# Another order of the same steps on every engine of a four-stage graph network kernel

## What is computed

```python
h = relu(layernorm(x)); x = x + L0(h, adj)   # two layers: softmax of h.h^T, masked; three products with weights
h = relu(layernorm(x)); x = x + L1(h, adj)   # two layers: two bilinear scores, masked exp; one linear product
h = relu(layernorm(x)); x = x + L2(h, adj)   # attention, 12 heads of 32, bias 2*adj, output projection
h = relu(layernorm(x)); x = x + L3(h, adj)   # attention, 12 heads of 32, masked by adj
```

## Time and profile before

| what | value |
|---|---|
| time, median of 3 runs | 2900.89 us (2900.38 to 2901.71) |
| the profiled execution's own time | 2899.22 us |
| its span, first to last instruction | 2897.5 us |
| granted TensorE clock, mean | 0.995 |
| PE busy | 2794.9 us (96%) |
| DVE busy | 2424.7 us (84%) |
| ACT busy | 2116.5 us (73%) |
| POOL busy | 846.4 us (29%) |

### The profile page before, as it was taken

How to read it: one execution, slowest core, us unless ns; L and a number is a source line. 1 busy time by engine, 2 the same in 40 slices (tenths; PEclk the granted TensorE clock), 3 DMA queues, 4 the chain that set the end, 5 groups by cost and what they waited for, 6 DMA issues and landing times.

```text
span 2897.5 us, 87504 instructions
## 1 busy us (share of the span) xinstructions
PE 2794.9 (96%) x33735; PEld 2130.6 (74%) x33735; DVE 2424.7 (84%) x7450; ACT 2116.5 (73%) x6036; POOL 846.4 (29%) x1227
## 2 busy tenths in 40 slices
PE   6999999999999999999999999999999999999998
PEld 4777777777777777777777777677777777777787
DVE  5788888888888888898888888888888888888884
ACT  5677777777777777777677777777777777777763
POOL 0133233233233233233232332232332332332331
PEclk8999999999999999999999999999999999999999
DMA  6132232232232232232232322322322222322222
GB/s 220 21 56 45 50 54 45 52 53 46 52 55 44 52 54 45 52 56 43 51 49 46 55 47 49 54 46 48 57 45 49 57 47 47 57 44 49 54 50 42
DMA packets 458222, 154.85 MB, mean 53 GB/s; under 512 B 415312, under 2 KB 457808, under 8 KB 457808
## 3 DMA queue, kind: packets, MB, share of 16 engines
q1 hardware_dynamic: 457808, 149.25, 27.2%
HBM read 35.92 MB, written 12.58 MB: 17 GB/s over the span
## 4 chain that ended last, share of the span: by engine, by line
PE 64%; DVE 17%; DMA 8%; issue 4%; POOL 4%; SPq 2%; ACT 1%; DVEq 0%; POOLq 0%; ACTq 0%
PE bank_c L374 23%; PE bank_a L374 13%; PE bank_b L374 13%; DMA pt_halves<-prob_halves 7%; PE bank_c L548 4%; DVE score L1064 4%; PE bank_b L406 3%; POOL prob_halves L1220 2%; DVE neg_head_max L1069 2%; PE bank_c L420 2%; SPq L315 2%; PE bank_b L413 1%; DVE scaled_b L995 1%; PE bank_b L420 1%; POOL rstd_c L1171 1%
## 5 line engine op out<-in xcount | busy, mean ns | idle before, releaser
L1220 POOL TENSOR_TENSOR prob_halves<-prob,prob_halves 128x384 f16<-128x384 f32 x512 | 473.7, 930 | 597.7 <-DVE prob_halves L1079 597.6
L785 ACT ACTIVATE prob<-score,neg_head_max 128x128 f32<-128x128 f32 x1536 | 494.8, 390 | 56.5 <-DVE neg_head_max L1069 54.6
L1064 DVE SCALAR_TENSOR_TENSOR score<-bank_c,bias 128x384 f32<-128x384 f32 x512 | 281.8, 550 | 212.8 <-PE bank_c L548 202.7
L374 PE MATMUL bank_c<-htc_hi,w_lo 128*128 128x128 f16 x2304 | 405.4, 219 | 0.0
L374 PE MATMUL bank_c<-htc_lo,w_hi 128*128 128x128 f16 x2304 | 405.4, 219 | 0.0
L374 PE MATMUL bank_c<-htc_hi,w_hi 128*128 128x128 f16 x2304 | 405.4, 219 | 0.0
L374 PE MATMUL bank_a<-w_hi,hta_hi 128*128 128x384 f16 x1152 | 375.4, 326 | 0.7
L374 PE MATMUL bank_a<-w_lo,hta_hi 128*128 128x384 f16 x1152 | 375.4, 326 | 0.0
L1069 DVE TENSOR_REDUCE neg_head_max<-score 128x3 f32<-128x384 f32 x512 | 280.0, 547 | 2.4
L374 PE MATMUL bank_a<-w_hi,hta_lo 128*128 128x384 f16 x1152 | 250.3, 326 | 0.0
L374 PEld LDWEIGHTS bank_c<-htc_lo,w_hi 128*128 128x128 f16 x2304 | 225.4, 98 | 13.8
(11 more groups left out here) (202 smaller groups left out, 8991.2 us busy)
## 6 DMA issues: line engine op xcount, KB each, us to landing
x_in<-x SPq DMA_DIRECT2D x64, 192.0 KB, 2.4
out<-y_out SPq DMA_DIRECT2D x64, 192.0 KB, 2.4
pt_halves<-prob_halves SPq DMA_TRANSPOSE x512, 2.8
w_stage<-w_t SPq DMA_DIRECT2D x11, 576.0 KB, 5.7
adj_in<-adj SPq DMA_DIRECT2D x64, 64.0 KB, 2.1
adj_t<-adj_turned SPq DMA_DIRECT2D x64, 64.0 KB, 2.2
score<-w_t SPq DMA_DIRECT2D x4, 576.0 KB, 7.3
prob<-w_t SPq DMA_DIRECT2D x4, 576.0 KB, 7.5
```

The costliest lines, as they stand in the source:

```text
L374: mm = nc.tensor.matmul(out_ap, a, b, start=first and i == 0, stop=last and i == len(pairs_of) - 1, skip_group_check=True)
L785: ex = nc.scalar.activation(prob[:, j, c, :], score[:, j, c, :], ACT.Exp, bias=neg_head_max[:, j, c:c + 1])
L1064: V.scalar_tensor_tensor(score[:, j, :, :], chunked(c_banks[j][:, 0:D]), scale, bias[:, :].unsqueeze(1).to_broadcast([128, CHUNKS, 128]), ...
L1220: P.tensor_tensor(prob_halves[:, j, 1, :, :], prob[:, j, :, :], prob_halves[:, j, 0, :, :], ALU.subtract)\
```

## The change

The same steps run; `ORDER`, `FIRST`, `SPLITS`, `WARM_FIRST` and `WARM_LAST` are written anew. `WARM_START` stays 110. No generator, buffer, wait or instruction form changes. The idle matmuls are 225 and 806 (232 and 745 before).

The period's string of PE begins at another place. Turned so that both begin at the same step, with the moved letters apart, they read as follows (`-` before, `+` after):

```diff
-b y a yyyyyyyxx c   xxxxxabx tx yyyy b yaybyay wwtbwwwwxxaxx cc xx c x cacbax c x ccaw cwyybwwbwwc
+b y   yyyyyyyxx a c xxxxxabt xx yy a y b yybyay wwtbwwwwxxaxx ccc xxx cabacxx ccc aw cwyybwwbwwc
```

The diff:

```diff
 ORDER = {
-    "pe": "cwyybwwbwwcbyayyyyyyyxxcxxxxxabxtxyyyybyaybyaywwtbwwwwxxaxxccxxcxcacbaxcxccaw",
-    "act": "gwenwmicnwbjccjccjnbcbfjcgkbxccbakeknakeewebcwcwccqbbfagexipbaeieib",
-    "dve": "bbpbipppaipbabbbabcjbcacccjbccbjhaccnabhaqbkacbabaxnbhhakbbabbbaacaccbcchcchaczhhzbbpaazaa"
-           "apaaipbabxp",
-    "pool": "bmbhmnqahhbhhhhhaac",
-    "sp": "lsttttttttu",
+    "pe": "byyyyyyyyxxacxxxxxabtxxyyaybyybyayywwtbwwwwxxaxxcccxxxcabacxxcccawcwyybwwbwwc",
+    "act": "micnwbcwjcjnccjbnqbgjfckcbxckbaekcakeewebcwcwnccbbgfaxeibpiaeeigbwe",
+    "dve": "bpppaipbbbbbcjabcaacjccjcbcbccaqaaabkbabbhcxbhakbnbhabbbanahcccbcchacchaczahhzbbpazapaabaa"
+           "ipbaxbpbaip",
+    "pool": "bhnhhhhhaaqmcbbmahh",
+    "sp": "slutttttttt",
 }
 SPLITS = {
-    "act": [(0, -1), (0, -1), (0, -1), (0, -1), (0, -1), (0, -1), (0, -1), (0, 24),
-            (0, 27), (0, 45), (0, 46), (0, 48), (0, 59), (1, 8), (1, 16), (1, 18),
-            (1, 27), (1, 45), (2, 22)],
-    "dve": [(0, -1), (0, -1), (0, -1), (0, -1), (0, -1), (0, -1), (0, 4), (0, 72),
-            (0, 78), (0, 78), (0, 100), (1, 13), (1, 21), (1, 26), (1, 68), (1, 68),
-            (1, 68), (2, 16), (2, 65)],
+    "act": [(0, -1), (0, -1), (0, 44), (0, 51), (0, 52), (0, 61), (1, 4), (1, 9),
+            (1, 29), (1, 29), (1, 29), (1, 42), (1, 44), (1, 48), (2, 9), (2, 24),
+            (2, 24), (2, 66), (3, 33)],
+    "dve": [(0, -1), (0, -1), (0, 84), (0, 95), (1, 13), (1, 16), (1, 20), (1, 41),
+            (1, 63), (1, 63), (1, 63), (1, 79), (1, 95), (2, 16), (2, 58), (2, 69),
+            (2, 70), (3, 41), (4, 14)],
...
 }
```

More of the change, by code:

```diff
@@ L22 @@
 ORDER = {
-    "pe": "cwyybwwbwwcbyayyyyyyyxxcxxxxxabxtxyyyybyaybyaywwtbwwwwxxaxxccxxcxcacbaxcxccaw",
-    "act": "gwenwmicnwbjccjccjnbcbfjcgkbxccbakeknakeewebcwcwccqbbfagexipbaeieib",
-    "dve": "bbpbipppaipbabbbabcjbcacccjbccbjhaccnabhaqbkacbabaxnbhhakbbabbbaacaccbcchcchaczhhzbbpaazaa"
-           "apaaipbabxp",
-    "pool": "bmbhmnqahhbhhhhhaac",
-    "sp": "lsttttttttu",
+    "pe": "byyyyyyyyxxacxxxxxabtxxyyaybyybyayywwtbwwwwxxaxxcccxxxcabacxxcccawcwyybwwbwwc",
[4 more added lines that the diff above has]
+    "sp": "slutttttttt",
 }
 FIRST = {
[5 rows of a table removed]
[5 rows of a table added]
 }
 SPLITS = {
-    "act": [(0, -1), (0, -1), (0, -1), (0, -1), (0, -1), (0, -1), (0, -1), (0, 24),
-            (0, 27), (0, 45), (0, 46), (0, 48), (0, 59), (1, 8), (1, 16), (1, 18),
-            (1, 27), (1, 45), (2, 22)],
-    "dve": [(0, -1), (0, -1), (0, -1), (0, -1), (0, -1), (0, -1), (0, 4), (0, 72),
-            (0, 78), (0, 78), (0, 100), (1, 13), (1, 21), (1, 26), (1, 68), (1, 68),
-            (1, 68), (2, 16), (2, 65)],
-    "sp": [(0, -1), (0, -1), (0, -1), (0, 9), (0, 10), (1, 5), (1, 5), (1, 7),
-            (1, 7), (2, 10), (3, 5)],
+    "act": [(0, -1), (0, -1), (0, 44), (0, 51), (0, 52), (0, 61), (1, 4), (1, 9),
[4 more added lines that the diff above has]
+            (2, 70), (3, 41), (4, 14)],
+    "sp": [(0, -1), (0, -1), (0, 3), (0, 3), (0, 10), (1, 10), (1, 10), (2, 5),
+            (2, 5), (2, 10), (3, 5)],
 }
@@ L50 @@
 WARM_FIRST = {
-    (0, 69): 49, (1, 1): 8, (1, 9): 13, (1, 13): 11, (1, 29): 38, (1, 40): 11, (1, 53): 12, (1, 56): 11,
-    (1, 69): 22, (2, 11): 6, (2, 33): 16, (2, 38): 6, (2, 40): 6, (2, 47): 8, (3, 1): 8, (3, 13): 7,
+    (0, 57): 17, (0, 64): 8, (0, 72): 6, (0, 75): 14, (1, 11): 11, (1, 18): 39, (1, 25): 12, (1, 42): 13,
+    (1, 45): 11, (1, 57): 23, (2, 0): 12, (2, 22): 8, (2, 25): 5, (2, 27): 14, (2, 36): 12, (2, 64): 8,
+    (3, 0): 12,
 }
 WARM_LAST = {
[4 rows of a table removed]
[4 rows of a table added]
 }
```

## The result

The changed kernel takes 2907.71 us (median of 9 runs, 2903.61 to 2911.62) against 2901.16 us of the kernel before on the same chip (9 runs); the ratio is 1.0023, 95% interval 1.0013 to 1.0033. It is slower by 0.23%. Forecast was 2893.9 us.

A forecast was written before the change was run, and what follows sets the result against it. PE, busy 96%, was taken as the bound. Terms -2 -4 +4 +0 -7 +0 = -9, with 2 taken back: -7 from the profiled 2899.22 gives 2892.2, the median 1.7 above: 2893.9 us; range 2880 to 2907.

The forecast's parts named there:

- POOL's masks: Two masks on POOL before the root of L2's chain to stage b: just fit; if late, up to 0.3 a graph.
- the chain of L2 to the nodes of stage b: From L2's projection to stage b's nodes: var_eps_ab leaves the chain, -4 us; ends -4 and +18.
- rival C: DVE's dense stretch overflows between L3's and L2's scores (first place), or POOL's masks before the root (second): 2912 us, chance 0.18.
- The start: Graph 0's statistics before most weight splits: lead 10, less 1.5 for splits and 1.5 for PE's clock, -7 us; ends 0, -11.
- The quads of L2: PE's quads 0 and 1 of L2 put off, same steps before the fourth quad: -2 us; ends 0 and -48.
- SyncE's wait for PE at L315: Sign of a right forecast: SyncE's wait for PE before the transposes (L314 in the kernel before) still near 330 us.
- Third L3 quad: PE's third L3 quad beside the first two frees quad 2's buffer earlier, which was no bound: 0.
- L3's high halves: L3's high halves later on DVE, feeding PE's L3 quad steps over 10 us later; cover holds: 0.
- SyncE: Store, load and turned adjacency's load still come behind the last L2 transpose on the same queue: 0.
- DVE's dense stretch: DVE's 14.9 us from L3's to L2's scores, 0.17 us left there: 0; ends -6 to +24 us.
- y and the mask before the end of stage a: DVE's y and stage b's mask on the way to hta_lo, hidden except in undisturbed graphs: +4 us; ends 0, +15.
- The 4.4 us: Estimated cost of half-rate PE clock for 27 products of graph 0's first layer, 0.16 us each, part beside missing weights.

The follow-up runs named there:

- after: The changed kernel itself, against the kernel before: 2907.71 us, ratio 1.0023.
- e1: Against after: on POOL the root of L2's norm again ahead of the no-edge and upper-triangle masks of stage b; 2910.46 us, ratio 1.0023 to the kernel before.
- e7: Against after: on POOL the roots of L2's norm and of stage b's second layer ahead of both masks; 2890.8 us, ratio 0.9972 to the kernel before.
- e12: Against e8: splits and idle matmuls of the first periods placed as in the kernel before; 2904.7 us, ratio 1.0012 to the kernel before.
- e8: Against after: POOL as in e7, DVE as in e2, SyncE as in e6; 2889.84 us, ratio 0.9971 to the kernel before.
- e11: Against e8: no idle matmuls in the first four periods, the 110 at the very start kept; 2888.06 us, ratio 0.9958 to the kernel before.
- e4: Against the kernel before: weight splits and first periods' idle matmuls placed as in after, steps in the old order; 2900.59 us, ratio 0.9982.
- e5: Against the kernel before: POOL's two masks alone moved to their place in after, ahead of the root of L2's norm; 2959.25 us, ratio 1.0194.
- e10: Against e8: PE's edge product of stage a moved ahead of L2's fourth quad; 2896.6 us, ratio 0.9979 to the kernel before.
- e13: Against e8: as e10, and both parts of the next product ahead of the head outputs' turn; 2902.3 us, ratio 1.0007 to the kernel before.
- e6: Against after: SyncE's three other transfers in their old order behind the fourth transpose, store last; 2905.07 us, ratio 1.0024 to the kernel before.
- e2: Against after: DVE's low halves of stage b's projections again ahead of the small operations; 2907.8 us, ratio 1.0018 to the kernel before.

## Why the prediction was wrong

**The step that failed** is the price of POOL's masks in the term "the chain of L2 to the nodes of stage b" (-4 us), put at nothing with "the root of stage ab that precedes them is some 1.5 us ahead, so they just fit". The masks did not fit. By the rows of *after*, the root of stage ab starts at 1396.54 and L2's variance is ready at 1398.04, 1.50 us later, as forecast. Into these 1.50 us the root of stage ab and two masks had to go: starts at 1396.54, 1397.17, 1397.90 and then the root of L2 at 1398.32, 1.78 us. The prediction knew the length of one mask (0.65) and bounded the loss at 0.3 us a graph, which was right (0.24); it took the good end because "just fit" was read as zero. It also counted only one root behind the masks; e1 showed a second with no room either. The masks' price was 15 us (e7 against *after*), not 0. The -4 beside it, for var_eps_ab, came: without the masks the distance is 0.81 in place of 0.86 us (e7), 3 us. The term as a whole was +11 (0.86 to 1.05; 18.6 to 29.5 us in PEld's row) in place of -4. These 15 us account for the 14 by which the forecast missed. The prediction had named it as the second place of rival C, with 0.18 for both places; C's time, 2912, is nearer than the forecast's, but its first place and its reason did not come.

With the masks out of the way e7 comes out 8 us under the kernel before, where the forecast, which had them at nothing, was 7. That this fits so well is luck in part: the start gave 5 to 6 us more than its term, and e7's middle is 2 to 7 us longer than the two profiles of the kernel before have it.

**The start**: forecast -7, lead 10 less 1.5 for splits and 1.5 for the clock. Measured -13.5 in the profile and -12 in e12 against e8. The lead at the second graph was 12.1 in place of 10, and nothing was taken back: e11 shows no cost of the clock. This term was mis-sized, its mechanism right. The statistics at 8.65 and the next graph's L696 at 47.94 are both a little ahead of the signs that the prediction gave (9 to 10, 49 to 53).

**The quads of L2** (-2): the fourth quad starts 7.90 us after the first L3 quad step ends, in the mean of graphs 5 to 59, against 7.78 before; the four profiles of the old order (with e4 and e5) give 7.78 to 7.99, the eight of the new order (without e10 and e13) 7.82 to 7.98. No gain and no loss that stands out. The prediction's 6.7 us from the first issue to the fourth landing is built from medians and one graph; the mean of the kernel before is 3 x 1.47 + 3.22 = 7.6, so the mean turn, and not only the slow one, is late for PE's 6.9. The reasoning on the order held: the same steps stand between, so the quads' new places change nothing. One sign of it was forecast wrongly: SyncE's wait for PE at L315 is 221.9 us and not near 330. The halves come 1.7 us later per graph, but still ahead of PE's release: the first transpose starts 0.08 us behind it in both kernels.

**Third L3 quad, L3's high halves, SyncE** (0 each): no distance of PE outside the turn changed by these, and e6 confirms SyncE.

**DVE's dense stretch** (0, first place of rival C): held. The scores of L3 and L2 in *after*, beside the earlier trace rows:

```profile
1407.54 0.56 DVE L1065 SCALAR_TENSOR_TENSOR score<-bank_c,bias 128x384 f32<-128x384 f32 x1 [0.47 <-PE bank_c L549]
...
1422.53 0.56 DVE L1065 SCALAR_TENSOR_TENSOR score<-bank_c,bias 128x384 f32<-128x384 f32 x1 [0.48 <-issue]
```

DVE still stands 0.48 us before L2's scores (0.17 before): it has more room there, not less. The period did pass the 43.8 us that the prediction gave as a sign of C, but not with the wait at L457 or the full DVE that was to go with it. Of the 3.09 us before L3's scores 0.47 are left, because the turned attention's copy, which waits for PE, now stands there; it cost nothing.

**y and the mask before the end of stage a** (+4): the next product of PE starts within 0.01 us of where it did. It was hidden; 0.

**What the signs gave.** About -12 for the start and +15 for the masks is +3; measured was +6.6. The 3 to 4 us left are also what e12 shows over the kernel before. By the table they lie in the turn: the rest of the period is the same in e7, e8 and before (35.34, 35.34, 35.31 and 35.34), DVE's 0.07 us of e2 being made up for there by what var_eps_ab gives. The turn is 8.24 to 8.29 against 8.15 and 8.23, within its spread; what makes it so stays open.

The rule of the Trainium skill that the prediction weighed (TensorE: Matmul & The Clock Gate, Part 1: an array that was idle runs its first matmuls at half rate) agrees with the granted clock in e11, 0.83 against 0.91. The 4.4 us that the prediction estimated from it do not show in the time of e11; what covered them, no run shows.

## What to carry to other kernels

Where an engine's order is written out, "just fits" is not zero: add up the starts of all operations between two releases, on the engine with 29% load too, and set the sum beside the time to the hundredth. A small filler step belongs behind every step that a chain waits for: if it is taken from ahead of one and lands ahead of the next (e1), nothing is won, and one may conclude wrongly that it was harmless. On PE, look for it in the rows of the weight loads: there the price of the masks stood in the first profile, 10.9 us, where the rows of the matmuls had lost it. And a wait that is last in a chain whose later links are covered by the work behind it isn't free room: moving that cover ahead of the wait moves the wait (e10, e13).

## What the hardware showed

A DVE operation that starts within a POOL mask takes nearly twice as long. L912 (two operands in SBUF) in *after* from 400 to 2580 us, and the same line in e7, where POOL is idle at that time:

```profile
L912 DVE SCALAR_TENSOR_TENSOR junk_a<-attn_a,ident x99: 281/293/543, 407.1 to 2560.8; 128x128 f32<-128x128 f32 x99
```

```profile
L911 DVE SCALAR_TENSOR_TENSOR junk_a<-attn_a,ident x100: 280/288/295, 404.6 to 2567.4; 128x128 f32<-128x128 f32 x100
```

543 ns against 288: 48 of the 99 start while the second mask runs, and take 0.54 us on the mean; the other 51 take 0.29. In graph 29 it is the one that starts at 1397.97 while the mask of 1397.90 runs to 1398.36. The Trainium skill, SBUF — State Buffer, "Who interferes with whom", says that a DVE instruction with two SBUF inputs contends with a GpSimd instruction that reads SBUF, and that the later one is blocked until the first ends. The trace agrees in kind: the operation ends at 1398.51, 0.15 us behind the mask, and so do all 48 (0.14 to 0.15). It does not agree to the hundredth: had the operation only begun at 1398.36, its 0.28 us would end it at 1398.64. It was not on the path here, but the root behind the mask was: its own time went from 547 to 607 ns (medians of e7 and *after*), a quarter of the 0.24 us. It starts while L912 still runs; whether that is the cause, no run shows.
